# Queries of two batches in one product of 224 columns, in the third layer's attention

## What is computed

```python
def _L2_xattn_ref(x, context, Wq, Wk, Wv, Wo, bo):
    q = (x @ Wq.T).reshape(b, nq, H, DH)            # H = 16, DH = 64
    k = (context @ Wk.T).reshape(b, nk, H, DH)
    v = (context @ Wv.T).reshape(b, nk, H, DH)
    sim = jnp.einsum('bihd,bjhd->bhij', q, k) * SCALE
    attn = jax.nn.softmax(sim, axis=-1)
    out = jnp.einsum('bhij,bjhd->bihd', attn, v).reshape(b, nq, H * DH)
    return out @ Wo.T + bo
...
x = x + _L2_xattn_ref(_layernorm(x, axis=-1), ctx_1024, ...)
```

## Time and profile before

| | |
|---|---|
| median of three runs | 2617.29 us |
| profiled execution, device time | 2616.1 us |
| its span, first to last instruction | 2614.4 us |
| mean granted TensorE clock | 0.94 |
| TensorE busy | 2278.6 us, 87% |
| VectorE busy | 1292.3 us, 49% |
| ScalarE busy | 1045.0 us, 40% |
| third layer's attention in the span | about 1156 to 1896 us |

### The profile page before, as it was taken

How to read it: one execution, slowest core, us unless ns; L and a number is a source line. 1 busy time by engine, 2 the same in 40 slices (tenths; PEclk the granted TensorE clock), 3 DMA queues, 4 the chain that set the end, 5 groups by cost and what they waited for, 6 DMA issues and landing times.

```text
span 2614.4 us, 45875 instructions
## 1 busy us (share of the span) xinstructions
PE 2278.6 (87%) x15822; PEld 1763.3 (67%) x15822; DVE 1292.3 (49%) x3990; ACT 1045.0 (40%) x2806; POOL 258.4 (10%) x297
## 2 busy tenths in 40 slices
PE   5888885999968499949999999999869948989888
PEld 3777774677746467637777777878647637777755
DVE  5777773222244622264454444444542267777723
ACT  3776771222223112214444444444302227777721
POOL 0000000111132024200000000000014300000010
PEclk8999996999979789969999999999969969999999
DMA  6777765122236212310000000000042168877600
GB/s 194 193 189 188 188 161 232 65 81 86 74 105 197 111 41 65 88 50 13 7 17 11 13 11 17 7 11 10 5 188 64 55 185 194 190 189 190 149 11 21
DMA packets 149438, 252.60 MB, mean 97 GB/s; under 512 B 14736, under 2 KB 124640, under 8 KB 146544
## 3 DMA queue, kind: packets, MB, share of 16 engines
q1 hardware_dynamic: 138560, 220.31, 31.0%
q0 software_dynamic: 10656, 29.37, 3.6%
HBM read 191.04 MB, written 58.59 MB: 95 GB/s over the span
## 4 chain that ended last, share of the span: by engine, by line
PE 72%; DVE 14%; issue 6%; ACT 4%; DMA 3%; SPq 0%; DVEq 0%; ACTq 0%; POOLq 0%
PE bank L1635 8%; PE bank L955 6%; PE bank L924 6%; PE bank L1665 6%; PE bank L838 5%; PE bank L834 5%; PE bank L1690 5%; PE bank L912 4%; PE bank L869 4%; PE bank L825 3%; PE bank L1678 3%; DVE arena L1164 3%; PE bank L1942 2%; PE bank L849 2%; PE bank L1928 2%
## 5 line engine op out<-in xcount | busy, mean ns | idle before, releaser
L924 PE MATMUL bank<-ident,arena 112*125 112x112 f32 x2352 | 370.2, 275 | 1.1 <-ACT arena L1219 1.0
L924 PEld LDWEIGHTS bank<-ident,arena 112*125 112x125 f32 x2352 | 341.1, 188 | 39.7 <-issue 3.0
L1212 ACT ACTIVATE arena<-arena,mx 112x375 f32<-112x375 f32 x512 | 309.1, 605 | 138.5 <-DVE mx L1164 136.2
L1164 DVE CUSTOM_DVE_ANT_0 arena<-bank,maskf 112x375 f32<-112x375 f32 x512 | 274.7, 542 | 92.0 <-PE bank L907 79.3
L907 PE MATMUL bank<-kS,qS 128*112 128x376 f32 x512 | 238.0, 466 | 33.3 <-DMA kS<-key_halves 20.5
L955 PE MATMUL bank<-arena 125*32 125x112 f32 (+1 forms) x4608 | 202.0, 264 | 57.5 <-DVE arena L1185 28.3
L1176 DVE TENSOR_REDUCE mx<-bank 112x1 f32<-112x375 f32 x256 | 128.6, 543 | 246.7 <-PE bank L912 246.3
L955 PEld LDWEIGHTS bank<-arena 125*32 125x32 f32 (+1 forms) x4608 | 147.3, 118 | 145.1 <-issue 67.9
L1635 PE MATMUL bank<-arena 128*128 x532 | 231.8, 559 | 3.2 <-ACT arena L1739 3.2
L1185 DVE COPY arena<-bank 125x336 f32<-125x336 f32 x448 | 214.5, 502 | 32.2 <-PE bank L924 32.2
L1212 ACT ACTIVATE arena<-bank,mx 112x375 f32<-112x375 f32 x272 | 155.8, 574 | 175.3 <-DVE mx L1176 151.0
(11 more groups left out here) (246 smaller groups left out, 3665.2 us busy)
## 6 DMA issues: line engine op xcount, KB each, us to landing
kS<-key_halves SPq DMA_DIRECT2D x256, 188.0 KB, 5.3
qS<-query_halves SPq DMA_DIRECT2D x128, 224.0 KB, 4.6
arena<-in_ctxT SPq DMA_DIRECT2D x64, 376.0 KB, 4.6
key_halves<-arena SPq DMA_DIRECT2D x64, 376.0 KB, 4.7
arena<-in_f_out SPq DMA_DIRECT2D x21, 768.0 KB, 4.5
query_halves<-arena SPq DMA_DIRECT2D x32, 448.0 KB, 3.9
arena<-in_f_up SPq DMA_DIRECT2D x4, 2816.0 KB, 19.0
arena<-results SPq DMA_DIRECT2D x20, 448.0 KB, 8.1
```

The lines of the kernel that those rows point to most:

```text
L924: m = pe.transpose(bank[2 + g % 2][0:KT, k * S:(k + 1) * S], pr[:, g % t.NR, k * KT:(k + 1) * KT], ident[0:S, 0:S])
L1164: dve.tensor_tensor_reduce(sm[:, g % 2, :], bank[g % 2][0:S, 0:SK], maskf[:, :], 1.0, 3e38, ALU.add, ALU.min, mx[:, g % t.NR:g % t.NR + 1])\
L1212: act.activation(pr[:, g % t.NR, :], src, ACT.Exp, bias=mx[:, g % t.NR:g % t.NR + 1], scale=-1.0, accum_out=row_sum(t, b)[:, h:h + 1]).the ...
```

## The change

The queries of two batches are made together. The tokens of batches b and b + 1 lie side by side in `xnT`, so one matmul takes 224 columns; a product is then two tiles of 128 inner features for two batches and fills the same 448 columns of a bank. There are four of them, cost 1.5 each, in the list of every even batch, and none in that of an odd one; the sum of the costs of a batch's list becomes 25.66 or 19.66 where it was 23.26. With four buffers for queries (in the same 3584 columns of the arena), two can be written while two are read. VectorE's evacuation writes both batches' buffers in one instruction. The first scores of a batch wait for the query evacuations of its pair.

```diff
@@ proj
         q = [(gen("q", o), 0.45 * self.QG, 0) for o in range(0, self.NO, self.QG)]
+        if self.halves:
+            q = [(gen("q", o), 1.5, 0) for o in range(0, self.NO, 2)] if b % 2 == 0 else []
@@ build
-        qmv = lambda t, b: qflat[:, b % t.NV * (2 * 16 * S // t.NV):][:, 0:2 * 16 * S // t.NV].rearrange("p (h t) -> p h t", t=S)
+        qmv = lambda t, b: qflat[:, b % 4 * t.NO * S:(b % 4 + 1) * t.NO * S].rearrange("p (h t) -> p h t", t=S)
@@ att_tensor, gen
+                elif kind == "q" and t.halves:
+                    for j in range(2):
+                        for c in range(ND):
+                            m = pe.matmul(dst[:, j * 2 * S:(j + 1) * 2 * S], w[0][:, c, (o + j) * P:(o + j + 1) * P],
+                                          xnT[:, c, b * S:(b + 2) * S], start=(c == 0), stop=(c == ND - 1))
@@ att_tensor, scores
-                        freed_all(pe, t, "q", b)
+                        freed_all(pe, t, "q", b // 2 * 2)
@@ att_vector, gen
-                    ins = dve.tensor_scalar(qmv(t, b)[:, o:o + t.QG, :],
-                                            src[:, 0:t.QG * S].rearrange("p (o t) -> p o t", t=S),
+                    both = qflat[:, b % 4 * t.NO * S:(b % 4 + 2) * t.NO * S].rearrange("p (e h t) -> p e h t", e=2, t=S)
+                    ins = dve.tensor_scalar(both[:, :, o:o + 2, :],
+                                            src[:, 0:4 * S].rearrange("p (j e t) -> p e j t", j=2, t=S),
                                             qscale, None, ALU.mult)
```

## The result

The changed kernel takes 2640.31 us (median of four runs, 2637.82 to 2652.2). The kernel before takes 2616.2 us (median of four) on the same chip. The ratio is 1.0101, 95% interval 1.007 to 1.0132: 1% slower, or 26 us by the ratio. The profiled execution took 2637.82 us with a span of 2636.1, 21.7 more than before. The forecast was 14.6 more. Five further runs of the change on another chip (e8) have a median of 2640.88 us (2638.69 to 2648.78), ratio 1.0103.

What follows compares the result with a forecast made beforehand. TensorE was taken as the bound. Merging -9.0, uncovered halving +19.1 and empty last pairs +4.5 sum to +14.6 us, 2630.7 against the profiled 2616.1, so 2631 as the median of runs; range 2621 to 2645.

Steps and rivals of the forecast that it cites:

- the forecast's own spread: The narrower interval around the forecast of 2631 us: 2625 to 2637 us, chance 0.68.
- The bound: In the third layer's attention TensorE is the bound: each us it saves or stands is a us of the span.
- Part 1: Query products in the loop and ahead of it: fewer, longer matmuls, 0.189 us a record, save 9.0 us.
- The rival that merging saves nothing: Query matmuls: the 224-column record takes 0.224 us, so merging gives 0; sum +23, 2640 us; chance 0.03.
- Ahead of the loop: Before the first scores: two more query products go ahead of the keys, 16 records, 3.0 us on the path.
- Part 2: First pair of eight odd-target windows: first key product waits for the halving, 2.35 us (window 0: 2.6), 19.1 in all.
- Rival (c): First key product: halves are there when it is issued, so no pauses; -4.5 us, 2613; chance 0.05.
- (d): First key product: half of each stall (1.2 us) is hidden by a delay in the scores; +5, 2622; chance 0.09.
- Part 3: Last pair of odd-target windows loses its value product and runs empty: 0.65 us each, seven new windows, 4.5 us.
- my sentence that the layer norm's steps come one slot earlier at no cost: Layer norm steps in the windows: one slot earlier, on VectorE, which is half idle; cost nothing.
- Rival (a): Clock falls in the new pauses, 1.7 us each: all eight +14, 2645 us; half of them 2638; chance 0.15.
- my own three signs of being wrong: Profile after: halving waits under 1 us, dips in the clock row, or 224-column records over 0.2 us apart.

Runs made afterwards that it cites:

- e8: The changed kernel as it is, run five more times on another chip with a second profile; median 2640.88 us, ratio 1.0103.
- e3: The changed kernel with the same plan, but each query matmul of 224 columns made as two of 112, one per batch; 2648.26 us, ratio 1.0124.
- e1: The changed kernel, but with two of the next pair's four 224-column query products put in each window; 2613.88 us, ratio 0.9994.
- e5: The changed kernel with the cast of each context's halving made twice; 2658.07 us, ratio 1.0156.
- e6: The kernel before the change with the cast of each context's halving made twice; 2614.7 us, ratio 0.9996.
- e4: The changed kernel, but the last value product of an odd target batch is kept for the last pair; 2633.17 us, ratio 1.007.
- e7: From e1, with first queries evacuated before the weights are halved, and a planner cost of 3.0 on the last batch's context step; 2610.35 us, ratio 0.998.
- e2: The changed kernel, but an odd batch's context step costs 3.6 in the planner, so its keys start from the second pair; 2619.54 us, ratio 1.0013.

## Why the prediction was right, point by point

**The number.** The direction was forecast, and the largest terms are where they were said to be. The size was short: 2640.3 us lie in the range of 2621 to 2645, but above 2637, the end of the forecast's own spread, to which I had given 0.68. The range held because its upper end was made for eight falls of the clock at 1.7 us. What filled it was something else, three falls of 1.3 to 1.6 us and several small terms, so that the median lies inside is in part luck.

**The bound.** TensorE decided. Every wait that the trace shows inside the windows turned up in their length.

**Part 1, merging.** Spacing forecast 0.189, measured 0.190; saving 1.12 for two batches, measured 1.06. The rival that merging saves nothing fell (e3). The formula of the Trainium skill that I had set beside it, page "TensorE: Matmul & The Clock Gate", section "Back-to-back issue gap", would have had a ratio of one to two between the spacings; 0.112 to 0.190 is what stands. I had left out that the section gives the formula for the gap of a single isolated matmul, and says itself that at small N it counts too little in a stream with weight loads.

**Ahead of the loop.** Forecast +3.0, measured +3.5. The 16 records stood in the half-clock stretch behind the wait and took 5.3 us to the first key product where 3.0 were counted, and the key products behind them 8.54 where they had taken 10.30. That the sum came out so near is luck: both sides were off by about 2 us.

**Part 2, the pause.** Forecast 2.35 us in seven windows and 2.6 in window 0, 19.1 in all; measured 2.45 each in seven (3.12 us from L931 to L841 less the 0.67 without a wait; 2.21 are idle time, since the last transpose record ends only 0.91 behind the start of L931) and 2.61 in window 0, waits of 18.1 us. The 0.1 us that each was short is the step from VectorE's end to TensorE's start. I had taken 0.05 us, from a wait for L1071; behind the subtraction it is 0.15 (1281.45 to 1281.60), and the trace of before has that value too, behind four of its waits, that of L876 for L1135 among them (VectorE ends at 1896.29):

```profile
1896.44 0.57 PE L876 MATMUL bank<-ident,xn 112*128 112x112 f32 x4 [4.64 <-DVE xn L1135]
```

The cause of the pause is shown twice: it goes with cover (e1) and grows by what VectorE is given to do (e5 against e6). Rival (c), that the halves would be there in time, and (d), that half of the pause would be hidden, are out: none of it was.

**Part 3, the empty pair.** Forecast 0.65. In the change the first scores of window 3 (L919 at 1320.16) show the same 1.44 as the earlier trace rows, and e4 gets 0.6 a window back.

**What was missed.** The sum of 14.6 was short by 7. Of this the two falls of the clock in windows 0 and 6 are 2.7; the windows 2 to 13 cost 2.1 us a pair and not 1.8, which with 0.3 in windows 0 and 14 makes 2.1 in all, a third of it the 0.1 us of each pause; the part ahead 0.5; and window 15 3.6 where 0.65 were forecast, so 2.9. There my sentence that the layer norm's steps come one slot earlier at no cost failed: in window 15 nearly all pairs are empty, so TensorE reaches the transposes of the normalised rows sooner than VectorE is through with the steps in its list:

```profile
1891.69 0.91 PE L931 MATMUL bank<-ident,arena 112*125 112x112 f32 x6
1894.02 0.57 PE L883 MATMUL bank<-ident,xn 112*128 112x112 f32 x4 [1.42 <-DVE xn L1143]
1895.86 1.39 PE L962 MATMUL bank<-arena 125*64 125x112 f32 x12
```

It waits 1.42 us, and behind it the clock stands at half for 3.4 us (the stretch from 1894.80 above), the value products taking 1.39 for 0.80. In the kernel before the same product (L876 there) comes a pair later and waits for nothing. In e1 it waits 1.4 us again and in e7, where the steps behind the keys have their old slots, not at all. The profiles share out the length of window 15 up to its last pair: 25.5 us before, 26.4 with the wait alone (e4), 27.0 with the empty pair ahead of it too (e1, e3, e5), 28.6 with the fall as well (the change); 0.5 more lie in the last scores, which are stretched behind an empty pair. The rest of the program, in which nothing was changed, took 1.1 us less than before, and with it the terms come to the span's 21.7 within 0.2 us.

**Rival (a), the clock.** I gave it 0.15 and 1.7 us a fall for the case of half or all pauses. It came true in part and in every profile with eight pauses of this length: behind two to four of them, 1.3 to 1.6 us for a fall of 3.4 us. The term was not nought and belonged in the forecast, and one of my own three signs of being wrong came up with it: the clock row shows dips, where I had it at 1.00 up to 1896. The chance was too low also because I had read too few rows. The three pauses of 1.78 us that passed without a fall have a fourth beside them in the same layer, of 1.83 us, at which the clock did fall:

```profile
804.60 0.94 PE L876 MATMUL bank<-ident,xn 112*128 112x112 f32 x4 [1.83 <-DVE xn L1135]
...
804.70:808.00 3.30, 3.30 (x10) 2.49 (x11) 1.24 (x5) 1.34 (x4) 0.79 (x1) 0.50 0.48 185
```

The range up to 2645 holds the median; three of the nine runs of the change lie above it (2647.7, 2648.8 and 2652.2), which more falls would explain, though no profile of those runs shows them.

## What to carry to other kernels

Before work is taken from a saturated engine, look at what that work hides on another engine: here 3.67 us of matmuls covered 2.3 us of VectorE's halving, and to merge them saved 1.1 us for two batches and uncovered 2.45. Merge for the cheaper instruction, but leave a share of it in the place where something must be waited for (e1, e7), and re-read the planner's slots, since every step behind the edit moves with the sum of the costs. An empty slot is no cure either: the wait that goes from one semaphore came back at the next instruction that needs VectorE (e2). And look in the plan, or in the trace, whether a cost put into the planner moved the step that it was meant to move (e7).

## What the runs showed of the hardware

**A short pause can cost the clock, and need not.** A pause of TensorE of 2.2 to 2.6 us in an otherwise dense stream had a half clock of 3.4 us (once 6.8) with it in 13 of 34 cases, and pauses of 2.8 to 3.2 us (e5) in five of eight. The 1.42 us before L883 in window 15, which stand among short pairs, had one in two of the six profiles that have them (both of the change itself); a single one of 1.85 us (e2) had none.

The second layer, which no edit touches, says more, as it stands in all ten profiles. Its three pauses of 1.78 us in a row (847.01 in the trace of before is the second) never had a fall. The one at 804.60, 1.83 us in the trace of before and 1.77 to 3.9 us in the ten, had one each time. The one of 3.04 us had one in seven profiles and none in three (the change, e4 and e7). So the length of a pause alone does not tell whether the clock falls, and the same pause can have a fall in one execution and none in the next. What decides it is open. Whether the spread of the change's runs comes from it (14 us in four and 10 in five, beside 9 us in 23 runs of before and 6 in eleven of e1) was not tried by itself.

The Trainium skill, page "TensorE: Matmul & The Clock Gate", section "HAM oscillation — how this bites in real kernels", warns of idle gaps between bursts of matmuls, after which the next burst starts at the low clock. That they are paid in the work behind them agrees with the 4.60 us for 3.31 shown above; its example has waits of 3 to 5 us, and here a fall stood at a pause of 1.83.

**From VectorE's end to TensorE's start** 0.15 us pass behind the subtraction, eight times in the change, and 0.05 behind the evacuation of a query bank (1169.22 to 1169.27 before).

**Spacing.** An fp32 record of 224 columns follows the one before after 0.190 us, and one of 112 columns after 0.112, in the same place of the same program (e3): 1.7 times for twice the columns.
